# A transposed batch without its side buffer, and the order of ScalarE's work at the head of an expert stage

## The chip, the cores and the metric

The kernel runs on one core of a Trainium2 chip. The metric is the device time of one execution in microseconds, here the median of three runs. The core has five engines: TensorE (PE in the profile), VectorE (DVE), ScalarE (ACT), GpSimd (POOL) and SyncE (SP), whose queue issues all the transfers of this kernel. Each engine works through its own instructions in program order and waits at semaphores for the others.

## The reference, cut to what matters

```python
xn = layernorm(x)                                  # x: (16, 512, 128) fp32
h  = xn @ fc_w.T + fc_b
for _ in range(8):                                 # dt = 1/8
    h = h + dt * (sigmoid(alpha) * 0.5 * (adj @ h - h) + h @ w_eff - h + xn)
x  = x + h
z  = layernorm(x)
p  = softmax(z @ router_w.T)                       # 8 experts, the 2 best kept
out = z
for e in range(8):
    out = out + combine[:, e] * (gelu(z @ w1[e] + b1[e]) @ w2[e] + b2[e])
return x + out
```

## The kernel before

The 16 batches are taken in 8 groups of two (GB = 2). An iteration g first does the graph part of group g (eight Euler steps folded into products with powers of two matrices, and the second layer norm), and then the expert stage of group g - 1. Iteration 0 has no expert stage, iterations 1 to 6 are alike, iteration 7 is the last with a graph part, and after it comes the expert stage of group 7 alone. This text numbers the expert stages 1 to 8; stage k works on group k - 1.

An expert stage has 16 items, eight experts for each of the two batches. Names for item i:

- U(i): three TensorE matmuls, z times the first weights (split in a high and a low part), into one of three PSUM banks (lines 1129 to 1131).
- G(i): GELU on ScalarE into `hid` (line 610).
- S(i): VectorE multiplies by the token's routing weight into `scaled`, one of three buffers (line 989).
- H(i): ScalarE rounds `scaled` to its high part in `scs` (line 482, called by `item_high`).
- L(i): VectorE subtracts, giving the low part (line 678, called by `item_low`).
- D(i): TensorE adds w2 times both parts to the sum bank: two matmuls that need H(i) (line 1306) and one that needs L(i) (line 1313, "the low matmul").

TensorE's order is U0 to U5, D0, U6, D1 and so on (LAG = 5); U(i) for i of 3 and more waits for G(i - 3), whose bank it takes. ScalarE's order is G0 G1 H0 G2 H1 G3 H2 ... VectorE's is S0 S1 L0 S2 L1 ... `hid` has two buffers.

In between stand other things. In the stages 1 to 7 the layer norm's result z for the next group is written tile by tile: VectorE scales the four tiles of the first batch behind items 5 and 6, ScalarE those of the second batch (`scale_z`, line 592) behind items 6, 7, 8 and 9. When the last is done, SyncE writes z to memory and reads it back in blocks (lines 345 and 351); VectorE transposes these (`turn_z`, line 961) after item 15, and high and low parts go to `zT`, from which the next stage's U and the router's logits read. The second batch goes to a side buffer `zT_next`, and ScalarE copies it to `zT` (`move_zt`, line 578) at the start of the next iteration. In stage 7 nothing goes through memory: TensorE transposes z's two batches behind items 10 and 12 of its order (`Z_AT`), ScalarE and VectorE take the parts at once, and TensorE computes the logits before D13. The routing follows on VectorE, and stage 8 begins with TensorE replicating routing rows (line 1277) as soon as ScalarE has copied the result (`combT`).

VectorE turns the first batch's sum (`turn_y`, line 978) behind S11 and L10, and GpSimd then adds the residual (line 447).

Of the kernel before, what the change touches and what calls it, by code (L numbers as in the profile page):

```python
# [29 lines left out]
F32R = mybir.dt.float32r  # L30
# [5 lines left out]
P = 128  # L36
# [8 lines left out]
def build(nc, x, adj, alpha, w, d, fc_w, fc_b, router_w, w1, b1, w2, b2, comb_rows, x0_rows, z_rows, res_rows, out):  # L45
    B, N, D = x.shape
    E = router_w.shape[0]
    NT = N // P
# [12 lines left out]
    with ctx:  # L61
        def sb(name, shape, dt=FP32):
            return ctx.enter_context(nc.sbuf_tensor(name, shape, dt))

        def sem(name):
            return ctx.enter_context(nc.semaphore(name))
# [47 lines left out]
        resq = sb("resq", [P, GB, N])  # L114
        zt = sb("zt", [P, GB, N])
        zT = sb("zT", [P, 2, GB, N], F32R)
        zT_next = sb("zT_next", [P, 2, N], F32R)
        rt = sb("rt", [P, 6, T, E])
        rm = sb("rm", [P, 10, T])
        cc = sb("cc", [P, T, 4, E])  # L120
        lgT = cc[:, :, :, :].rearrange("p t k e -> p t (k e)")
        combT = sb("combT", [P, H], F32R)
        comb_out = sb("comb_out", [P, H])
        work = sb("work", [P, 5, N])
        hid = work[:, 0:2]
        scaled = work[:, 2:5]
        Lnat = work[:, 0:4]
        w12_raw = work[:, 0:4].rearrange("p (k r) n -> p k (r n)", k=2).rearrange("p k (e c) -> p k e c", c=D)
        w_raw = work[:, 4, 0:2 * P].rearrange("p (k c) -> p k c", c=P)
# [61 lines left out]
        h8_mm, x1_add = sem("h8_mm"), sem("x1_add")  # L191
        z_ready, res_ready = sem("z_ready"), sem("res_ready")
        zt_mm, zt_hi, zt_lo = sem("zt_mm"), sem("zt_hi"), sem("zt_lo")
        zt_moved = sem("zt_moved")
        z_kept, zq_in, z_turned = sem("z_kept"), [sem(f"zq_in{b}") for b in range(GB)], sem("z_turned")
        lg_mm, rt_own, rt_pre, rt_tanh, comb_ready = (sem(n) for n in ("lg_mm", "rt_own", "rt_pre", "rt_tanh", "comb_ready"))
        rep_mm = sem("rep_mm")
# [25 lines left out]
        H8_BANK = [4, 5, 6, 7]  # L223
        REP_ITEMS = [0, 2, 6, 8, 14]
        REP_BANK, REP_PE = [3, 7], 6
        Z_SCALE, Z_AT = 5, [10, 12]
        BY_PE = GROUPS - 2
        ROUTE_AT = [0, 1, 3, 4]
        UP_BANK, SUM_BANK = [4, 5, 6], [0, 1]
# [18 lines left out]

            return R * (2 * b + half)

        def zt_part(s, b):

            return zT_next[:, s, :] if b == GB - 1 else zT[:, s, b, :]

        def wait_low(engine, h, i):

# [223 lines left out]
        def _(act):  # L480
            def high(dst, src):
                return nc.scalar.activation(dst, src, ACT.Copy)  # L482
# [82 lines left out]
            def high_z(turn, b, banks=ZT_BANK):  # L565

                act.wait_ge(zt_mm, GB * turn + b + 1)
                high(zt_part(0, b), bank[banks[b]][:, :]).then_inc(zt_hi, 1)

            def high_turned_z(g, b):  # L570
                act.wait_ge(z_turned, GB * (g - 1) + b + 1)
# [2 lines left out]
            def route_tanh(h):  # L574
                act.wait_ge(rt_pre, h + 1)
                nc.scalar.activation(rm[:, 4, :], rm[:, 3, :], ACT.Tanh, scale=0.5).then_inc(rt_tanh, 1)

            def move_zt(h):

                act.wait_ge(zt_lo, GB * h + GB)  # L580
                high(zT[:, :, GB - 1, :], zT_next[:, :, :]).then_inc(zt_moved, 1)

            def copy_comb(h):

# [3 lines left out]
            def scale_z(g, b, t):  # L588
                if t == 0:
                    act.wait_ge(ln_rstd[1], 2 * g + 2)  # L590
                k = GB * t + b
                last = nc.scalar.activation(z[:, t, b, :], x1[:, t, b, :], ACT.Identity,
                                            bias=shift[:, 1, k:k + 1], scale=rstd[:, 1, k:k + 1])
                if t == NT - 1:
                    last.then_inc(z_ready, 1)
# [7 lines left out]
            def experts(h, g=None, more=False):  # L603

                for i in range(ITEMS):
                    act.wait_ge(up_mm, ITEMS * h + i + 1)
                    if i >= 2:
                        act.wait_ge(sc_ready, ITEMS * h + i - 1)
                    e = i % E
                    nc.scalar.activation(hid[:, i % 2, :], bank[UP_BANK[i % 3]][:, :], ACT.Gelu,  # L610
                                         bias=cols[:, B1_COL + e:B1_COL + e + 1]).then_inc(gelu_done, 1)
                    if i == 1 and g is None:
                        copy_comb(h)
                    if i >= 1:
                        item_high(h, i - 1)
                    if Z_SCALE < i <= Z_SCALE + NT and g is not None:
                        scale_z(g, 1, i - Z_SCALE - 1)
                    if i - 1 in Z_AT and g is not None and not more:
                        high_z(1, Z_AT.index(i - 1))
                    if i == ITEMS - 4 and not more:  # L620
                        copy_sum(h, 0)
                item_high(h, ITEMS - 1)
                if more:
                    high_turned(g + 1)
                if not more:
                    copy_sum(h, 1)
                if more:
                    for b in range(GB):
                        high_turned_z(g, b)
                if g is not None and not more:  # L630
                    route_tanh(g)

            def iteration(g, first=False, final=False):
                if not first:
                    move_zt(g - 1)
                    high_gt(g, 3, 3)
                    route_tanh(g - 1)
                for p in range(2):
                    act.wait_ge(q_ready, T * g + NT * (p + 1))
                    high(y2s[:, 0, 2 * p:2 * p + 2], Q[:, 2, 2 * p:2 * p + 2]).then_inc(y2_hi, 1)  # L640
                    if p == 1 and not first:
                        copy_comb(g - 1)
                    if p == 0 and not final:
                        scale_x0(g + 1)
                        high_x0(g + 1)
                for t in range(NT):
                    act.wait_ge(y1_add, NT * g + t + 1)
                    high(y1s[:, 0, t], y1[:, t]).then_inc(y1_hi, 1)
                if not final:
                    copy_x(g + 1)  # L650
                if first:
                    high_x0t(g + 1)
                    for k in range(2):
                        high_gt(g + 1, k, k)
                    for b in range(GB):
                        high_z(0, b, ZT_FIRST)
                    high_gt(g + 1, 2, 2)
                else:
                    experts(g - 1, g, not final)
                    if not final:  # L660
                        for k in range(3):
                            high_gt(g + 1, k, k)
# [2 lines left out]
            with act.Fori(1, GROUPS - 1) as g:  # L665
                iteration(g)
            iteration(GROUPS - 1, final=True)
            move_zt(GROUPS - 1)
            experts(GROUPS - 1)


# [1 line left out]
        def _(dve):  # L673
# [280 lines left out]

            def low_z(g, b, banks=ZT_BANK):
                dve.wait_ge(zt_hi, GB * g + b + 1)
                low(zt_part(1, b), bank[banks[b]][:, :], zt_part(0, b)).then_inc(zt_lo, 1)

            def turn_z(g, b):
                dve.wait_ge(zq_in[b], 64 * g)  # L960
# [19 lines left out]
            def scale_item(h, i, by_pe):  # L980

                dve.wait_ge(gelu_done, ITEMS * h + i + 1)
                if by_pe:
                    dve.wait_ge(rep_mm, i + 1)
                elif i in REP_ITEMS:
                    dve.wait_ge(rep_in[REP_ITEMS.index(i)], 16 * h + 16)
                if i >= 3:
                    wait_low(dve, h, i - 3)
                v.tensor_tensor(scaled[:, i % 3, :], hid[:, i % 2, :], bank[REP_BANK[i % 2]][:, :] if by_pe else rep(i),  # L989
                                ALU.mult).then_inc(sc_ready, 1)  # L990

            def item_low(h, i):
# [133 lines left out]
        def _(pe):  # L1126
# [119 lines left out]
                        if tiles[-1] == NT - 1:  # L1246
                            last.then_inc(done, 1)

            def logits(h):
                pe.wait_ge(zt_lo, GB * h + GB)  # L1250
                for b in range(GB):
                    for half in range(2):
                        first = P - R - quarter(b, half)
                        for s in range(2):
                            last = pe.matmul(bank[LG_BANK][:, 0:H], rts[:, first:first + P],  # L1255
                                             zt_part(s, b)[:, half * H:(half + 1) * H],
                                             start=(b + half + s == 0), stop=(b + half + s == 3))
                last.then_inc(lg_mm, 1)

# [21 lines left out]
            def experts(h, g=None, more=False):  # L1281

                for s in range(ITEMS + LAG):
                    if s < ITEMS:
                        b, e = s // E, s % E
                        if s >= 3:
                            pe.wait_ge(gelu_done, ITEMS * h + s - 2)
                        elif g is not None:
                            pe.wait_ge(x1_add, NT * g + s + 1)
                        elif UP_BANK[s] in OT_BANK:  # L1290
                            pe.wait_ge(out_add, 1 + GB * h)
                        if s == E:
                            pe.wait_ge(zt_moved, h + 1)
                        mm3(bank[UP_BANK[s % 3]][:, :], w1s[:, 0, e, :], w1s[:, 1, e, :],
                            zT[:, 0, b, :], zT[:, 1, b, :], True, True).then_inc(up_mm, 1)
                        if s == 1 and g is None:
                            pe.wait_ge(ct_high, h + 1)
                            replicate(h, 0)
                        if 1 <= s < REP_PE and g is None:
                            replicate(h, s)  # L1300
# [16 lines left out]
                    if s == ITEMS - 1 and not more:  # L1317
                        transpose_out(h, 0)
                    if s == ITEMS + 1 and g is not None and not more:
                        logits(g)  # L1320
                    if s >= ITEMS and more:
                        if s == ITEMS:
                            pe.wait_ge(x0_lo, GB * (g + 1) + GB)
# [91 lines left out]
```

## Time and profile before

| | |
|---|---|
| median of 3 runs | 533.34 us (532.8 to 533.89) |
| profiled execution | 534.12 us, span 532.0 us, mean granted TensorE clock 0.995 |
| TensorE busy | 517.8 us, 97% |
| VectorE busy | 439.0 us, 83% |
| ScalarE busy | 305.9 us, 57% |
| GpSimd busy | 112.0 us, 21% |
| GELU (line 610) | 128 of 0.679 us |
| high part of an item (line 482) | 132 of 0.629 us |
| low part of an item (line 678) | 132 of 0.739 us |

The span reaches from the first to the last instruction; the execution's own time has some two microseconds around it. Matmuls overlap at their ends, so TensorE's busy share says little of how close it is to its pace: the distance from one start to the next does. "L610" in a row is line 610 of the kernel. A row of a timeline has the start and the duration in microseconds, the engine, the line, the operation with output and input, the count of merged instructions, and in brackets the engine's idle time before it and who ended it.

### The profile page before, as it was taken

The page shows a single profiled execution, that of the slowest core. Times are in us where ns is not written, and L with a number is a line of the kernel's source. Part 1 is how long each engine was busy: PE and PEld are TensorE (multiplying, and loading weights), DVE is VectorE, ACT ScalarE, POOL GpSimd, SP SyncE. Part 2 cuts the span into 40 slices and gives each one's busy share as a digit, 9 for nine tenths or more (in the row PEclk, how much of TensorE's full clock was granted, in tenths as well). Part 3 has the DMA queues.
Part 4 walks back from the last instruction along what each step waited for, and adds up shares of the span by engine and source line. Part 5 has one row for each costly group of instructions (what it writes and reads, how often), then busy time and mean ns, then how long its engine had stood idle before and what let it go on. Part 6 is the DMA issues. An engine that isn't in the chain of part 4 may idle for free.

```text
span 532.0 us, 9196 instructions
## 1 busy us (share of the span) xinstructions
PE 517.8 (97%) x2799; PEld 453.6 (85%) x2799; DVE 439.0 (83%) x1012; ACT 305.9 (57%) x541; POOL 112.0 (21%) x174
## 2 busy tenths in 40 slices
PE   5999999999999999999999999999999999999796
PEld 4788997997799888998799878998899788988685
DVE  5888777779967997789967997789877996589985
ACT  6323434449635885459545884469545882159584
POOL 1204004204150412213240412222230412030100
PEclk9999999999999999999999999999999999999999
DMA  4040011099326972198327962298328841260151
GB/s 133 2 118 0 1 41 40 16 268 235 61 59 138 288 145 62 45 262 209 59 59 172 268 134 59 67 275 184 50 57 222 233 79 20 71 231 19 42 198 41
DMA packets 139359, 62.04 MB, mean 117 GB/s; under 512 B 102614, under 2 KB 133964, under 8 KB 137420
## 3 DMA queue, kind: packets, MB, share of 16 engines
q1 hardware_dynamic: 139340, 61.81, 46.7%
q8 instruction: 9, 0.15, 0.1%
q14 instruction: 10, 0.08, 0.0%
HBM read 47.90 MB, written 13.89 MB: 116 GB/s over the span
## 4 chain that ended last, share of the span: by engine, by line
PE 82%; DVE 8%; DMA 3%; ACT 2%; issue 2%; SPq 2%; POOL 1%; DVEq 0%; ACTq 0%; POOLq 0%
PE bank L1129 21%; PE bank L1131 21%; PE bank L1130 21%; PE bank L1306 10%; PE bank L1313 5%; DVE work L989 2%; DMA x0q<-x_rows 2%; DVE scs L678 1%; PE bank L1255 1%; ACT work L610 1%; DMA x_rows<-x 1%; SPq L338 1%; DVE bn L682 1%; DMA work<-in_adj_dram 1%; DVE Q L1097 1%
## 5 line engine op out<-in xcount | busy, mean ns | idle before, releaser
L678 DVE TENSOR_TENSOR scs<-work,scs 128x512 fp32r<-128x512 f32 x132 | 97.4, 739 | 1.9 <-ACT scs L482 0.5
L610 ACT ACTIVATE work<-bank,cols 128x512 f32<-128x512 f32 x128 | 86.8, 679 | 16.5 <-PE bank L1131 16.4
L482 ACT ACTIVATE scs<-work 128x512 fp32r<-128x512 f32 x132 | 83.0, 629 | 18.9 <-DVE work L989 17.5
L1306 PE MATMUL bank<-scs,w2s 128*128 128x512 f32 x256 | 80.7, 396 | 0.0
L1131 PE MATMUL bank<-M,GT 128*128 128x384 f32 x192 | 64.2, 335 | 0.0
L1129 PE MATMUL bank<-M,GT 128*128 128x384 f32 x192 | 64.2, 334 | 0.0
L1130 PE MATMUL bank<-M,GT 128*128 128x384 f32 x192 | 64.2, 334 | 0.0
L989 DVE TENSOR_TENSOR work<-work,GT 128x512 f32<-128x512 f32 x90 | 61.1, 685 | 3.2 <-issue 1.4
L423 POOL TENSOR_TENSOR mv<-bn 128x8 f32<-128x8 f32 x16 | 6.7, 418 | 240.6 <-DVE bn L682 240.6
L1306 PEld LDWEIGHTS bank<-scs,w2s 128*128 128x128 f32 x256 | 47.8, 188 | 10.8
L1129 PE MATMUL bank<-zT,w1s 128*128 128x512 f32 x128 | 52.1, 407 | 0.9 <-ACT work L610 0.4
L1313 PE MATMUL bank<-scs,w2s 128*128 128x512 f32 x128 | 51.1, 400 | 0.0
L1129 PE MATMUL bank<-LT,x0s 128*128 128x512 f32 x128 | 51.1, 399 | 0.0
L1131 PE MATMUL bank<-zT,w1s 128*128 128x512 f32 x128 | 50.8, 397 | 0.0
L1130 PE MATMUL bank<-zT,w1s 128*128 128x512 f32 x128 | 50.6, 395 | 0.0
L482 ACT ACTIVATE GT<-bank 128x512 fp32r<-128x512 f32 x36 | 21.1, 595 | 50.8 <-PE bank L1131 48.2
L1131 PE MATMUL bank<-LT,x0s 128*128 128x512 f32 x128 | 50.1, 391 | 0.0
L1130 PE MATMUL bank<-LT,x0s 128*128 128x512 f32 x128 | 49.9, 390 | 0.0
L1054 DVE TENSOR_TENSOR Q<-bank,bias 128x384 f32<-128x384 f32 x64 | 35.2, 550 | 17.6 <-PE bank L1131 17.5
L447 POOL TENSOR_TENSOR outs<-outs,resq 128x512 f32<-128x512 f32 x12 | 17.2, 1436 | 117.6 <-DVE outs L978 117.6
L678 DVE TENSOR_TENSOR GT<-bank,GT 128x512 fp32r<-128x512 f32 x36 | 24.5, 689 | 20.8 <-ACT GT L482 20.7
L1129 PEld LDWEIGHTS bank<-M,GT 128*128 128x128 f32 x192 | 36.0, 188 | 0.3
(193 smaller groups left out, 1227.5 us busy)
## 6 DMA issues: line engine op xcount, KB each, us to landing
GT<-comb_rows SPq DMA_DIRECT2D x8, 1536.0 KB, 7.1
Q<-comb_rows SPq DMA_DIRECT2D x16, 512.0 KB, 7.2
GT<-comb_rows SPq DMA_DIRECT2D x7, 1024.0 KB, 5.8
xn<-in_x_dram SPq DMA_DIRECT2D x16, 256.0 KB, 4.1
GT<-comb_rows SPq DMA_DIRECT2D x7, 512.0 KB, 4.4
res_rows<-scr SPq DMA_DIRECT2D x12, 256.0 KB, 2.6
x_rows<-x SPq DMA_DIRECT2D x12, 256.0 KB, 2.6
x0q<-x_rows SPq DMA_DIRECT2D x24, 128.0 KB, 4.0
```

The costliest lines, as they stand in the source:

```text
L423: nc.gpsimd.tensor_tensor(mv[:, n, 1, :], mean_e, mean_o, ALU.subtract)
L447: nc.gpsimd.tensor_tensor(turned, turned, resq[:, b, :], ALU.add).then_inc(out_add, 1)
L482: return nc.scalar.activation(dst, src, ACT.Copy)
L610: nc.scalar.activation(hid[:, i % 2, :], bank[UP_BANK[i % 3]][:, :], ACT.Gelu, bias=cols[:, B1_COL + e:B1_COL + e + 1]).then_inc(gelu_done, 1)
L678: return v.tensor_tensor(dst, src, hi.bitcast(FP32), ALU.subtract)
L989: v.tensor_tensor(scaled[:, i % 3, :], hid[:, i % 2, :], bank[REP_BANK[i % 2]][:, :] if by_pe else rep(i), ALU.mult).then_inc(sc_ready, 1)
L1054: v.tensor_tensor(Q[:, :, t, b, :], src, bias[:, t], ALU.add).then_inc(q_ready, 1)
L1129: pe.matmul(dst, wh, xh, start=start, stop=False)
L1130: pe.matmul(dst, wh, xl, start=False, stop=False)
L1131: return pe.matmul(dst, wl, xh, start=False, stop=stop)
L1306: pe.matmul(bank[SUM_BANK[b]][:, :], w2s[:, k, e, :], scs[:, i % RING, 0, :], start=(e == 0 and k == 0), stop=False)
L1313: pe.matmul(bank[SUM_BANK[b]][:, :], w2s[:, 0, e, :], scs[:, i % RING, 1, :], start=False, stop=(e == E - 1)).then_inc(down_mm, 1)
```

## The change

The side buffer and its copy go. In the inner iterations z's second batch is written straight into `zT`; in the last iteration, where `zT` is still being read, it goes to a part of `x0s` that is free by then. The room lets `work` grow from five to six tiles, and `hid` gets a third buffer. ScalarE's order at the head of a stage becomes G0 G1 G2 H0 H1 G3 H2 ..., and its four z tiles stand behind items 6, 8, 10 and 11.

```diff
-        zT_next = sb("zT_next", [P, 2, N], F32R)
...
-        work = sb("work", [P, 5, N])
-        hid = work[:, 0:2]
-        scaled = work[:, 2:5]
+        work = sb("work", [P, 6, N])
+        hid = work[:, 0:3]
+        scaled = work[:, 3:6]
...
-        Z_SCALE, Z_AT = 5, [10, 12]
+        Z_SCALE, Z_ACT, Z_AT = 5, [6, 8, 10, 11], [10, 12]
...
-        def zt_part(s, b):
-
-            return zT_next[:, s, :] if b == GB - 1 else zT[:, s, b, :]
+        def zt_part(s, b, last=False):
+
+            if last and b == GB - 1:
+                return x0s[:, s, 0:NT // 2].rearrange("p t b c -> p (t b c)")
+            return zT[:, s, b, :]
...
-            def move_zt(h):
-
-                act.wait_ge(zt_lo, GB * h + GB)
-                high(zT[:, :, GB - 1, :], zT_next[:, :, :]).then_inc(zt_moved, 1)
...
                     act.wait_ge(up_mm, ITEMS * h + i + 1)
-                    if i >= 2:
-                        act.wait_ge(sc_ready, ITEMS * h + i - 1)
+                    if i >= 3:
+                        act.wait_ge(sc_ready, ITEMS * h + i - 2)
                     e = i % E
-                    nc.scalar.activation(hid[:, i % 2, :], bank[UP_BANK[i % 3]][:, :], ACT.Gelu,
+                    nc.scalar.activation(hid[:, i % 3, :], bank[UP_BANK[i % 3]][:, :], ACT.Gelu,
                                          bias=cols[:, B1_COL + e:B1_COL + e + 1]).then_inc(gelu_done, 1)
                     if i == 1 and g is None:
                         copy_comb(h)
-                    if i >= 1:
+                    if i == 2:
+                        item_high(h, 0)
+                    if i >= 2:
                         item_high(h, i - 1)
-                    if Z_SCALE < i <= Z_SCALE + NT and g is not None:
-                        scale_z(g, 1, i - Z_SCALE - 1)
+                    if i in Z_ACT and g is not None:
+                        scale_z(g, 1, Z_ACT.index(i))
...
             def iteration(g, first=False, final=False):
                 if not first:
-                    move_zt(g - 1)
                     high_gt(g, 3, 3)
...
-                        if s == E:
-                            pe.wait_ge(zt_moved, h + 1)
                         mm3(bank[UP_BANK[s % 3]][:, :], w1s[:, 0, e, :], w1s[:, 1, e, :],
-                            zT[:, 0, b, :], zT[:, 1, b, :], True, True).then_inc(up_mm, 1)
+                            zt_part(0, b, g is None), zt_part(1, b, g is None), True, True).then_inc(up_mm, 1)
```

## Rows read from the trace of the kernel before

**Rows 1.** The page, busy time: us, share of the span, instructions.
```profile
PE 517.8 (97%) x2799; PEld 453.6 (85%) x2799; DVE 439.0 (83%) x1012; ACT 305.9 (57%) x541; POOL 112.0 (21%) x174
```

**Rows 2.** Timeline, TensorE, stage 2: start, duration (us), engine, line, operation.
```profile
176.14 0.40 PE L1129 MATMUL bank<-zT,w1s 128*128 128x512 f32 x1
...
179.34 0.39 PE L1131 MATMUL bank<-zT,w1s 128*128 128x512 f32 x1
179.84 0.50 PE L1129 MATMUL bank<-zT,w1s 128*128 128x512 f32 x1
...
196.23 0.49 PE L1313 MATMUL bank<-scs,w2s 128*128 128x512 f32 x1
```

**Rows 3.** Timeline, ScalarE, head of stage 2.
```profile
177.04 1.38 ACT L610 ACTIVATE work<-bank,cols 128x512 f32<-128x512 f32 x2 [1.51 <-PE bank L1131]
178.58 0.63 ACT L482 ACTIVATE scs<-work 128x512 fp32r<-128x512 f32 x1 [0.16 <-DVE work L989]
179.12 0.67 ACT L610 ACTIVATE work<-bank,cols 128x512 f32<-128x512 f32 x1
179.69 0.62 ACT L482 ACTIVATE scs<-work 128x512 fp32r<-128x512 f32 x1
```

**Rows 4.** Timeline, VectorE, stage 2.
```profile
177.85 1.31 DVE L989 TENSOR_TENSOR work<-work,GT 128x512 f32<-128x512 f32 x2 [0.16 <-ACT work L610]
179.25 0.69 DVE L678 TENSOR_TENSOR scs<-work,scs 128x512 fp32r<-128x512 f32 x1
179.85 0.68 DVE L989 TENSOR_TENSOR work<-work,GT 128x512 f32<-128x512 f32 x1
...
189.94 0.69 DVE L678 TENSOR_TENSOR scs<-work,scs 128x512 fp32r<-128x512 f32 x1
190.76 0.69 DVE L989 TENSOR_TENSOR work<-work,GT 128x512 f32<-128x512 f32 x1
...
194.38 1.79 DVE L678 TENSOR_TENSOR scs<-work,scs 128x512 fp32r<-128x512 f32 x1
```

**Rows 5.** Timeline, GpSimd, stage 2.
```profile
194.03 1.58 POOL L447 TENSOR_TENSOR outs<-outs,resq 128x512 f32<-128x512 f32 x1 [9.80 <-DVE outs L978]
```

**Rows 6.** Timeline, ScalarE, middle of stage 2.
```profile
187.65 0.63 ACT L482 ACTIVATE scs<-work 128x512 fp32r<-128x512 f32 x1
...
189.67 0.48 ACT L592 ACTIVATE scr<-Q,shift,rstd 128x128 f32<-128x128 f32 x1
190.05 0.67 ACT L610 ACTIVATE work<-bank,cols 128x512 f32<-128x512 f32 x1
```

**Rows 7.** Timeline, TensorE, stages 1 and 6.
```profile
116.81 0.40 PE L1129 MATMUL bank<-zT,w1s 128*128 128x512 f32 x1
...
137.16 0.51 PE L1313 MATMUL bank<-scs,w2s 128*128 128x512 f32 x1
...
412.84 0.40 PE L1129 MATMUL bank<-zT,w1s 128*128 128x512 f32 x1
...
432.93 0.48 PE L1313 MATMUL bank<-scs,w2s 128*128 128x512 f32 x1
```

**Rows 8.** Timeline, TensorE, stage 7 and head of stage 8.
```profile
487.45 0.60 PE L1263 MATMUL bank<-ident,scr 128*128 128x128 f32 x4
...
502.19 0.73 PE L1277 MATMUL bank<-combT,pick 128*128 128x256 f32 x4 [2.10 <-ACT combT L482]
```

**Rows 9.** Windows: us, busy and count by engine, granted clock, DMA share, GB/s.
```profile
502.20:506.30 4.10, 4.10 (x15) 3.50 (x16) 3.46 (x6) 2.25 (x4) 2.39 (x1) 0.58 0.26 72
```

**Rows 10.** Timeline, SyncE's queue, stage 2.
```profile
192.47 4.04 SPq L351 DMA_DIRECT2D x0q<-z_rows  x8
```

**Rows 11.** Timeline, VectorE, behind stage 2.
```profile
200.49 1.30 DVE L961 STREAM_TRANSPOSE zt<-x0q 128x512 f32<-128x512 f32 x2
```

**Rows 12.** Timeline, ScalarE, around the copy of line 581.
```profile
209.72 1.06 ACT L482 ACTIVATE zT<-zT_next 128x1024 fp32r<-128x1024 f32 x1
211.49 0.60 ACT L482 ACTIVATE GT<-bank 128x512 fp32r<-128x512 f32 x1 [0.70 <-PE bank L1131]
```

More of the change, by code:

```diff
@@ L193, in build @@
         zt_mm, zt_hi, zt_lo = sem("zt_mm"), sem("zt_hi"), sem("zt_lo")
-        zt_moved = sem("zt_moved")
         z_kept, zq_in, z_turned = sem("z_kept"), [sem(f"zq_in{b}") for b in range(GB)], sem("z_turned")
@@ L567, in high_z @@
                 act.wait_ge(zt_mm, GB * turn + b + 1)
-                high(zt_part(0, b), bank[banks[b]][:, :]).then_inc(zt_hi, 1)
+                high(zt_part(0, b, turn == 1), bank[banks[b]][:, :]).then_inc(zt_hi, 1)
             def high_turned_z(g, b):
@@ L667, in _ @@
             iteration(GROUPS - 1, final=True)
-            move_zt(GROUPS - 1)
             experts(GROUPS - 1)
@@ L956, in low_z @@
                 dve.wait_ge(zt_hi, GB * g + b + 1)
-                low(zt_part(1, b), bank[banks[b]][:, :], zt_part(0, b)).then_inc(zt_lo, 1)
+                last = banks is ZT_BANK
+                low(zt_part(1, b, last), bank[banks[b]][:, :], zt_part(0, b, last)).then_inc(zt_lo, 1)
             def turn_z(g, b):
@@ L988, in scale_item @@
                     wait_low(dve, h, i - 3)
-                v.tensor_tensor(scaled[:, i % 3, :], hid[:, i % 2, :], bank[REP_BANK[i % 2]][:, :] if by_pe else rep(i),
+                v.tensor_tensor(scaled[:, i % 3, :], hid[:, i % 3, :], bank[REP_BANK[i % 2]][:, :] if by_pe else rep(i),
                                 ALU.mult).then_inc(sc_ready, 1)
@@ L1247, in horner, with logits @@
                             last.then_inc(done, 1)
-            def logits(h):
+            def logits(h, final=False):
                 pe.wait_ge(zt_lo, GB * h + GB)
@@ L1255, in logits @@
                             last = pe.matmul(bank[LG_BANK][:, 0:H], rts[:, first:first + P],
-                                             zt_part(s, b)[:, half * H:(half + 1) * H],
+                                             zt_part(s, b, final)[:, half * H:(half + 1) * H],
                                              start=(b + half + s == 0), stop=(b + half + s == 3))
@@ L1319, in experts @@
                     if s == ITEMS + 1 and g is not None and not more:
-                        logits(g)
+                        logits(g, True)
                     if s >= ITEMS and more:
```

## The prediction

> **What bounds the kernel now.** I read the page's busy times first, then TensorE's timeline through one whole expert stage, then the timelines of ScalarE, VectorE and GpSimd beside it. TensorE is busy 517.8 of 532.0 us [rows 1], but that includes overlapping ends. The pace is in the starts: U0 starts at 176.14 and the last of U0 to U4's fifteen matmuls at 179.34 [rows 2], 14 steps of 0.229 us. TensorE is late where a step is longer, and I looked for such steps. In every expert stage 1 to 6 I found the same two. U5 begins at 179.84, not at 179.34 + 0.23 = 179.57: 0.27 us lost, and its first matmul takes 0.50 us instead of 0.39, another 0.11. The second is the low matmul of D11 (L1313) at 196.23, with 0.49 us again [rows 2].
>
> The first has a plain cause: U5 needs G2, and G2 (179.12 to 179.79) stands behind H0, which itself had to wait for S0 [rows 3]. The second needs VectorE: L11 starts at 194.38 and takes 1.79 us, to 196.17 [rows 4], and the matmul starts 0.06 later. L11 is long because GpSimd adds the residual from 194.03 to 195.61, released by VectorE's transpose just before [rows 5]. The transpose follows L10, so this overlap travels with VectorE's chain. VectorE works from L0 to L11 almost without a pause: scale and low part follow each other at 0.60 us (179.25 to 179.85); the one hole is before S10, at 190.76 instead of 189.94 + 0.60 = 190.54, so 0.22 us [rows 4], for G10, which ends at 190.05 + 0.67 [rows 6]. So the later limit of a stage is L11, whatever TensorE gains at U5. From U0 to D11's low matmul takes 20.35 us in stage 1 and 20.09 in stage 6 [rows 7]; the six are 20.35, 20.09, 20.35, 20.25, 20.14 and 20.09, mean 20.21. After it TensorE keeps its pace up to the next stage's U5.
>
> **The third GELU buffer and the new order.** From GELU 3 on ScalarE's order is what it was (G3, H2, G4, H3, ...), and H(i-2) had already waited for S(i-2), so the old condition on the second buffer never held G(i) longer. The only effect is at the head: G0 G1 G2 H0 H1 instead of G0 G1 H0 G2 H1. U2's last matmul starts 8 x 0.229 after 176.14, at 177.97, and takes 0.40; G2 can start at about 178.41 instead of 179.12, right behind G1 (177.04 + 1.38 = 178.42) [rows 2, 3]. It ends at 179.1, so U5 starts on time: gain 0.38 us at U5. H0, in exchange, starts a GELU later. From G2 to H1 the step is 0.57 (179.12 to 179.69) [rows 3], so H0 starts at 178.98 and ends 0.63 later at 179.61. L0 followed H0's end by 0.04 (178.58 + 0.63 = 179.21, L0 at 179.25) [rows 3, 4]; it now starts at 179.65, 0.40 later. VectorE has only S0 and S1 before it, done at 179.16 [rows 4], and S2 stands behind L0 in its order though G2 is ready early. So the whole chain L0, S2, L1, ... starts 0.40 later.
>
> **The moved z tiles.** ScalarE's four tiles go from items 6, 7, 8, 9 to 6, 8, 10, 11. A tile costs ScalarE 0.38 (189.67 to 190.05) [rows 6]. From H7 to G10 took 2.40 (187.65 to 190.05) [rows 6], with two tiles; with one it is 2.02, so G10 no longer holds S10: 0.22 back. Then G10, H9, a tile, G11 take 0.57 + 0.54 + 0.38 = 1.49, so G11 ends 2.02 + 1.49 + 0.68 = 4.19 after H7 starts, that is some 4.9 after S7 starts; VectorE would want it 8 x 0.60 = 4.8 after S7. S11 waits 0.1. Net of the two: 0.12 back.
>
> In stage 2, L11 then ends 0.40 - 0.12 = 0.28 later and D11's low matmul starts at 20.37 after U0. The head of the chain is now set by G2 and not by S0, so I expect 20.37 in all six stages against a mean of 20.21: 6 x 0.16 = 1.0 us slower. The 6 x 0.38 at U5 all goes into the longer wait at D11. Bounds: if S10's and S11's waits both vanish, 6 x 0.06 = 0.4; if neither does, 6 x 0.4 = 2.4.
>
> The last tile also ends 3.0 us later (it is two items of 1.2 and more behind), and with it the write of z to memory. The eight reads that turn z start at 192.47 and take 4.04 to issue [rows 10]; they move to 195.5 to 199.5. VectorE turns z at 200.49 and 201.14 [rows 11], so some 1.7 us lie between issue and the second use, where there were 4.7. A transfer in here may hold the second transpose by some tenths; the logits that need z come 7 us later (207.6), so I take nothing. Queued behind these reads on SyncE are the stores of the first output batch, which nobody waits for before the next stage.
>
> **The buffer removed.** The copy takes 1.06 us on ScalarE, but the high part behind it starts at 211.49 after 0.70 us of waiting for TensorE [rows 12]. It is hidden seven times and worth nothing; in stage 8 it stands before G0, long before the routing is ready. Should it have been a cover for something, 1.06 us per use is the most it could give back, and the 0.70 says it gives none. TensorE's removed wait had been met eight items before.
>
> **The last two stages.** In stage 7 TensorE transposes z's second batch behind D7, at 487.45 [rows 8]. The last tile ended 1.6 before that and will end 3.1 later, at about 488.9, so TensorE stops there for some 1.7 us. By itself this is hidden: the routing is the path, and TensorE waits 2.10 us for it at 502.19 [rows 8]. But ScalarE there has the copies of the transposed z and of the first sum between its GELUs and no idle time from H7 on, and one tile moves from before H7 to behind it. VectorE's chain begins 0.5 late (H0 again; here S0 was quicker than elsewhere) and waits 0.38 more at G12. So the routing ends 0.9 later: from 0.4 (the head alone) to 1.3 (two tiles). In stage 8, U2 stands behind the first replicated rows, so H0 behind G2 waits longer; TensorE needs S3 for the sixth replicated row, and I take 0.2 us, from 0 to 0.6.
>
> **Sum.** 1.0 + 0.9 + 0.2 = 2.1 us slower. The profiled execution took 534.12 us for its span of 532.0; it becomes 536.2. The median of the runs is 533.34, 0.8 below, so I forecast **535.4** (0.4% slower). No change means within 0.2% or 1.07 us, about what this kernel's measurement can tell.
>
> **Rivals.**
> (A) The forecast: the chain L0 to L11 is the limit and starts later. 0.58.
> (B) Faster: D11's wait moves with TensorE instead of with L11, so that the gap at U5 is truly gained. 6 x 0.38 = 2.3, less 1.1 in the last stages: 1.2 us faster, 532.1. It decides where D11's low matmul starts: if in stage 2 it comes before 20.0 us after U0, B holds. Against it: the start follows L11's end by 0.06. For it: the wait at U5 is real and the same in all stages. The Trainium skill (Perfetto Trace Analysis, Identifying Performance Opportunities) says that the same gap repeated on the engine that should be saturated can mean too few buffers; by that rule the third buffer gives these 2.3 us. The trace agrees on the gap, but shows a later one behind it. 0.08.
> (C) No change: VectorE swallows most of the 0.40, or z's tiles cost stage 7 only the head. 0.4 + 0.4 = 0.8 slower, 534.1. A z tile of VectorE that already waits for GpSimd in stages 1, 3 and 4 speaks for it, and the late ScalarE in stage 7 against it. 0.22.
> (D) The stop of 1.7 us in stage 7 halves TensorE's clock. After the 2.10 us wait the granted clock over 4.1 us was 0.58 [rows 9], so part of it at 1.2 GHz: (1 - 0.58) x 4.1 = 1.7 us of TensorE's time. The logits would come 1.7 later with 0.6 of slack: 1.1 more, 536.5. The Trainium skill (TensorE: Matmul & The Clock Gate, Part 1) has the throttled clock as the default that only activity lifts, which would make such a stop dear. The stop is shorter than that wait, so I hold it for unlikely. 0.12.
>
> **Range and chances.** A's own range is 534.4 to 536.6. With C's lower part and D, and the unknown costs, 532.9 to 537.3. Faster has B's 0.08; no change has C's 0.22; slower A and D, 0.70.
>
> **What would show it.** Right: U5 without a gap and its first matmul at 0.39 us; G2 directly behind G1; L0 0.40 later after U0; no wait before S10; D11's low matmul near 20.37 after U0 in all six stages, just behind L11, with a longer wait; a stop of TensorE before the second transposes of z in stage 7; the first replicated row 0.9 later than the stages' own delay explains. Wrong: D11's low matmul earlier than 20.0 after U0, or an L11 of 0.7 us because GpSimd's addition falls elsewhere, which would take 1.1 us off every stage's wait.

## The result and the profile after

The changed kernel takes 535.24 us (median of 6 runs, 534.98 to 535.8), the kernel before 533.25 (6 runs, 532.79 to 533.89). The ratio is 1.0037 with a 95% interval of 1.0026 to 1.0047: 0.4% slower, 2.0 us. The forecast was 535.4.

TensorE's timeline in stage 2 of the changed kernel (start, duration, line, operation; the lines have moved: a matmul of U is now L1125 to L1127, D's low matmul L1307):

```profile
175.30 0.40 PE L1125 MATMUL bank<-zT,w1s 128*128 128x512 f32 x1
...
178.50 0.39 PE L1127 MATMUL bank<-zT,w1s 128*128 128x512 f32 x1
178.73 0.39 PE L1125 MATMUL bank<-zT,w1s 128*128 128x512 f32 x1
...
188.86 0.50 PE L1125 MATMUL bank<-zT,w1s 128*128 128x512 f32 x1
...
195.66 0.50 PE L1307 MATMUL bank<-scs,w2s 128*128 128x512 f32 x1 [0.26 <-DVE scs L673]
```

U0 starts at 175.30. The last matmul of U4 starts at 178.50 and U5 follows at 178.73, one step of 0.23 later, and takes 0.39 us: the gap of [rows 2] is gone. D11's low matmul comes at 195.66, 20.36 after U0, where it was 20.09; it now waits so long that the profile lists the wait. A row in between shows a new small delay: U12's first matmul, at 188.86 and 0.50 us long, starts 0.06 after G9 ends (188.13 + 0.67, in ScalarE's rows below). The profile's chain of work that ended last has changed with it. Its shares of the span by engine:

```profile
PE 67%; DVE 19%; issue 6%; ACT 5%; POOL 1%; DMA 1%; DVEq 0%; SPq 0%; ACTq 0%; POOLq 0%
```

TensorE had 82% of this chain before, VectorE 8%. It now goes through VectorE's low parts (line 673, 9% of the span), which had 1%.

ScalarE, VectorE and GpSimd beside it, in the same stage:

```profile
176.20 2.06 ACT L605 ACTIVATE work<-bank,cols 128x512 f32<-128x512 f32 x3 [1.51 <-PE bank L1127]
178.16 1.14 ACT L482 ACTIVATE scs<-work 128x512 fp32r<-128x512 f32 x2
179.20 0.68 ACT L605 ACTIVATE work<-bank,cols 128x512 f32<-128x512 f32 x1
...
187.21 0.63 ACT L482 ACTIVATE scs<-work 128x512 fp32r<-128x512 f32 x1 [0.51 <-DVE work L985]
...
188.13 0.67 ACT L605 ACTIVATE work<-bank,cols 128x512 f32<-128x512 f32 x1
...
190.70 0.68 ACT L605 ACTIVATE work<-bank,cols 128x512 f32<-128x512 f32 x1
```

```profile
177.01 1.31 DVE L985 TENSOR_TENSOR work<-work,GT 128x512 f32<-128x512 f32 x2 [0.23 <-ACT work L605]
178.81 0.69 DVE L673 TENSOR_TENSOR scs<-work,scs 128x512 fp32r<-128x512 f32 x1 [0.48 <-ACT scs L482]
179.42 0.69 DVE L985 TENSOR_TENSOR work<-work,GT 128x512 f32<-128x512 f32 x1
...
189.51 0.68 DVE L673 TENSOR_TENSOR scs<-work,scs 128x512 fp32r<-128x512 f32 x1
190.11 0.68 DVE L985 TENSOR_TENSOR work<-work,GT 128x512 f32<-128x512 f32 x1
190.72 0.68 DVE L673 TENSOR_TENSOR scs<-work,scs 128x512 fp32r<-128x512 f32 x1
191.41 0.69 DVE L985 TENSOR_TENSOR work<-work,GT 128x512 f32<-128x512 f32 x1
...
193.82 1.78 DVE L673 TENSOR_TENSOR scs<-work,scs 128x512 fp32r<-128x512 f32 x1
```

```profile
193.48 1.58 POOL L447 TENSOR_TENSOR outs<-outs,resq 128x512 f32<-128x512 f32 x1 [10.89 <-DVE outs L974]
```

ScalarE runs three GELUs in one piece (176.20, three in 2.06 us) and then the high parts of items 0 and 1. Counted from U0, H0 starts at 2.86 instead of 2.44, and VectorE, which had S1 done at 178.32, is idle for 0.48 us before L0. L0 starts 3.51 after U0 instead of 3.11 [rows 4]: the 0.40 of the forecast. The hole before S10 is gone (189.51, 190.11, 190.72 are 0.60 apart); the one before S11 is new (191.41 instead of 191.32). L11 starts 0.28 later after U0 and takes 1.78 us, beside GpSimd's addition as before.

The six stages are now alike. Stage 1 and stage 6, U0 and D11's low matmul:

```profile
115.95 0.40 PE L1125 MATMUL bank<-zT,w1s 128*128 128x512 f32 x1
...
136.31 0.50 PE L1307 MATMUL bank<-scs,w2s 128*128 128x512 f32 x1 [0.27 <-DVE scs L673]
...
412.72 0.40 PE L1125 MATMUL bank<-zT,w1s 128*128 128x512 f32 x1
...
433.10 0.50 PE L1307 MATMUL bank<-scs,w2s 128*128 128x512 f32 x1 [0.27 <-DVE scs L673]
```

20.36 and 20.38 us, against 20.35 and 20.09 in [rows 7]. Over six iterations, from stage 1's U0 to stage 7's, the sum is 472.07 - 115.95 = 356.12 us, where it was 471.89 - 116.81 = 355.08: 1.04 us more.

Stage 7 and the head of stage 8, TensorE:

```profile
472.07 0.40 PE L1125 MATMUL bank<-zT,w1s 128*128 128x512 f32 x1
...
487.10 0.40 PE L1307 MATMUL bank<-scs,w2s 128*128 128x512 f32 x1
489.11 0.66 PE L1259 MATMUL bank<-ident,scr 128*128 128x128 f32 x4 [1.61 <-ACT scr L587]
...
503.25 0.73 PE L1273 MATMUL bank<-combT,pick 128*128 128x256 f32 x4 [1.44 <-ACT combT L482]
...
507.30 0.50 PE L1273 MATMUL bank<-combT,pick 128*128 128x256 f32 x2 [0.57 <-DVE work L985]
```

Behind D7 (487.10) TensorE stops for 1.61 us, until ScalarE's last z tile is done. The first replicated row comes 503.25 - 472.07 = 31.18 after stage 7's U0; it was 502.19 - 471.89 = 30.30. That is 0.88 more. In stage 8 there is a new wait of 0.57 us at 507.30, for S2.

TensorE's granted clock after both stops (windows, columns as in [rows 9]):

```profile
489.20:500.00 10.80, 10.11 (x53) 8.25 (x54) 10.03 (x23) 7.00 (x14) 0.00 (x0) 1.00 0.08 24
503.30:507.00 3.70, 3.43 (x17) 2.41 (x17) 2.36 (x5) 2.29 (x4) 2.39 (x1) 1.00 0.29 80
```

It stays at full speed, also in the stretch at the head of stage 8 where it was 0.58 before.

The reads that turn z, on SyncE's queue, and VectorE's use of them:

```profile
194.61 4.04 SPq L351 DMA_DIRECT2D x0q<-z_rows  x8
```

```profile
199.92 1.30 DVE L957 STREAM_TRANSPOSE zt<-x0q 128x512 f32<-128x512 f32 x2
```

The reads are issued 2.98 us later after U0 than in [rows 10], and VectorE's two transposes still start without a wait and follow L15 as in [rows 11].

### The profile page after: what moved, and what is told of

It is laid out like the page before. It is cut to its first block, busy times and chain, and to the rows that moved or that the text cites. A ratio compares the mean times of both kernels' runs of the same rounds, so it can differ in the third digit from the quotient of the medians.

```text
span 532.8 us, 9172 instructions
## 1 busy us (share of the span) xinstructions
PE 515.5 (97%) x2799; PEld 450.7 (85%) x2799; DVE 437.9 (82%) x1012; ACT 299.6 (56%) x533; POOL 107.6 (20%) x174
## 4 chain that ended last, share of the span: by engine, by line
PE 67%; DVE 19%; issue 6%; ACT 5%; POOL 1%; DMA 1%; DVEq 0%; SPq 0%; ACTq 0%; POOLq 0%
PE bank L1127 19%; PE bank L1125 19%; PE bank L1126 19%; DVE scs L673 9%; DVE work L985 5%; PE bank L1300 4%; PE bank L1307 2%; ACT scs L482 2%; ACT work L605 2%; PE bank L1251 1%; DVE scr L687 1%; DVE outs L974 1%; PE bank L1153 1%; POOL rstd L438 1%; DVE bn L677 1%
## 5 line engine op out<-in xcount | busy, mean ns | idle before, releaser
L1127 PE MATMUL bank<-M,GT 128*128 128x384 f32 x192 | 64.2, 335 | 0.0
L1125 PE MATMUL bank<-M,GT 128*128 128x384 f32 x192 | 64.2, 334 | 0.0
L1307 PE MATMUL bank<-scs,w2s 128*128 128x512 f32 x128 | 51.2, 400 | 1.6 <-DVE scs L673 1.6
L1125 PE MATMUL bank<-LT,x0s 128*128 128x512 f32 x128 | 51.1, 400 | 0.0
L1127 PE MATMUL bank<-LT,x0s 128*128 128x512 f32 x128 | 50.1, 392 | 0.0
L1125 PE MATMUL bank<-zT,w1s 128*128 128x512 f32 x120 | 48.3, 402 | 0.0
L1127 PE MATMUL bank<-zT,w1s 128*128 128x512 f32 x120 | 47.1, 393 | 0.0
L1126 PE MATMUL bank<-zT,w1s 128*128 128x512 f32 x120 | 46.9, 391 | 0.0
```

The source lines that it names most:

```text
L1125: pe.matmul(dst, wh, xh, start=start, stop=False)
L1126: pe.matmul(dst, wh, xl, start=False, stop=False)
L1127: return pe.matmul(dst, wl, xh, start=False, stop=stop)
L1307: pe.matmul(bank[SUM_BANK[b]][:, :], w2s[:, 0, e, :], scs[:, i % RING, 1, :], start=False, stop=(e == E - 1)).then_inc(down_mm, 1)
```

## The experiments

The first four were timed against 532.90 us, the median of 29 runs of the kernel before, the other four against 533.02 (23 runs). The changed kernel itself was timed only against the 533.25 above, so a difference from its 535.24 us carries the 0.2 to 0.4 us by which these medians of one kernel differ. The iteration times from the profiles do not.

**The old order at the head.**

```diff
-                    if i == 2:
-                        item_high(h, 0)
-                    if i >= 2:
+                    if i >= 1:
                         item_high(h, i - 1)
```

> The changed kernel with ScalarE's old order at the head of every stage (G0 G1 H0 G2 H1), all else as changed: third GELU buffer there but unused at the head, z tiles behind items 6, 8, 10, 11. My theory (H0 behind G2 starts VectorE's chain 0.40 us later): L0 at 3.1 to 3.2 us after U0 again instead of 3.51, the 0.38 us gap at U5 back, D11's low matmul near 20.1 after U0 instead of 20.36, so 6 x 0.26 = 1.5 us less in stages 1 to 6, 0.5 less in stage 7, and 0.2 in stage 8: 2.2 us faster than the changed kernel, 533.0, the same as before. Rival (the gain at U5 is real, the loss sits in z's moved tiles): slower than the changed kernel by 6 x 0.38 = 2.3, 537.5.

Measured: 533.09 us, 1.0002 of before (0.9993 to 1.0011). VectorE, then TensorE:

```profile
177.33 1.31 DVE L983 TENSOR_TENSOR work<-work,GT 128x512 f32<-128x512 f32 x2
178.72 0.69 DVE L671 TENSOR_TENSOR scs<-work,scs 128x512 fp32r<-128x512 f32 x1
```

```profile
179.32 0.50 PE L1123 MATMUL bank<-zT,w1s 128*128 128x512 f32 x1
...
487.72 0.55 PE L1257 MATMUL bank<-ident,scr 128*128 128x128 f32 x3 [0.81 <-ACT scr L587]
```

L0 starts right behind S1, 3.10 after U0 (175.62), and U5's first matmul is back at 0.50 us behind its gap. D11's low matmul starts 20.14 after U0. The six iterations take 354.76 us, against 355.08 before and 356.12 in the changed kernel. So this order, not the moved tiles, carries the loss of stages 1 to 6. The rival with 537.5 is out. The third GELU buffer is still there, and the gap at U5 is back: it was the new order that closed it, not the buffer by itself. In stage 7 the stop is still there but shorter (0.81 us, 487.72), and the first replicated row comes 30.67 after U0, 0.51 earlier than in the changed kernel.

**The old z tiles.**

```diff
-        Z_SCALE, Z_ACT, Z_AT = 5, [6, 8, 10, 11], [10, 12]
+        Z_SCALE, Z_ACT, Z_AT = 5, [6, 7, 8, 9], [10, 12]
```

> The changed kernel with ScalarE's z tiles behind items 6, 7, 8, 9 again. My theory: S10 waits 0.2 us for G10 again instead of S11 0.1 for G11, so D11's low matmul comes 0.1 later, at 20.47 after U0: 6 x 0.1 = 0.6 slower; in stage 7 the stop of 1.6 us before z's second transposes is gone and the routing comes 0.4 earlier: net 0.2 to 0.3 slower, 535.5, no measurable difference. Rival (the moved tiles are the loss): back to 533.3.

Measured: 535.91 us, 1.0052 of before (1.0039 to 1.0065). TensorE, stage 2's U0 and D11, and the first replicated row:

```profile
175.62 0.40 PE L1125 MATMUL bank<-zT,w1s 128*128 128x512 f32 x1
...
196.10 0.50 PE L1307 MATMUL bank<-scs,w2s 128*128 128x512 f32 x1 [0.30 <-DVE scs L673]
...
503.70 0.50 PE L1273 MATMUL bank<-combT,pick 128*128 128x256 f32 x2 [2.90 <-ACT combT L482]
```

D11's low matmul starts 20.48 after U0, 0.12 later than with the moved tiles. The six iterations take 356.76 us, 0.64 more than in the changed kernel. The first replicated row comes 503.70 - 472.92 = 30.78 after stage 7's U0, 0.40 earlier. Both sizes are the forecast's. The time is not: 0.7 us above the changed kernel, where 0.2 to 0.3 were expected. The low clock returned in stage 8, after a wait of 2.90 us for the routing (granted 0.65 from 503.7 to 508.6, with matmuls 0.43 us apart), and from the first replicated row to the last D it took 24.81 us instead of 24.39. The expectation had not priced these 0.4. With the new order in place, the moved tiles are thus a gain of 0.64 us in the six iterations and a loss of 0.40 in stage 7.

**Only the buffers.** The two edits above together. What stays of the change is the side buffer and its copy taken away, and the third GELU buffer, without the order that would use it.

> Both undone: the changed kernel with the old head order and the old z tiles, so that only the side buffer, its copy and TensorE's wait for it are gone. My theory (the copy was hidden): as before, 533.25 within 0.5 us, and the starts after U0 of all items as before. Rival (removing seven copies of 1.06 us helps): up to 7 us faster, 526.

Measured: 533.23 us, 1.0002 of before (0.9993 to 1.001). D11's low matmul starts 20.09 to 20.30 after U0 in the six stages, as before. The side buffer's copy was hidden: taking it away is worth nothing within the noise of 0.1%, and neither is the third GELU buffer by itself.

**The addition after L15, in the changed kernel.**

```diff
                 pool.wait_ge(resq_in, 64 * h + 64)
+                if b == 0:
+                    pool.wait_ge(sc_lo, ITEMS * h + ITEMS)
```

> The changed kernel, but GpSimd's residual addition for the first batch also waits for L15, so that it no longer runs beside L11. My theory (L11 is the later limit of a stage, and 1.1 of its 1.79 us is the addition): L11 takes 0.69, D11's low matmul follows its high ones at 19.9 to 20.0 after U0 instead of 20.36 and U5's gain is kept, 6 x 0.5 = 3.1 us faster than the changed kernel: 532.1, 0.2% faster than before. Rival (D11's low matmul waits for something else): no change, 535.2.

Measured: 532.13 us, 0.9987 of before (0.9979 to 0.9996). L11 on VectorE, then TensorE:

```profile
193.63 0.68 DVE L675 TENSOR_TENSOR scs<-work,scs 128x512 fp32r<-128x512 f32 x1
```

```profile
175.11 0.40 PE L1127 MATMUL bank<-zT,w1s 128*128 128x512 f32 x1
...
194.59 0.63 PE L1302 MATMUL bank<-scs,w2s 128*128 128x512 f32 x2
195.06 0.40 PE L1309 MATMUL bank<-scs,w2s 128*128 128x512 f32 x1
195.29 0.40 PE L1127 MATMUL bank<-LT,x0s 128*128 128x512 f32 x1
```

L11 takes 0.68 us, and D11's low matmul (195.06) follows its high ones by 0.47 without a wait, 19.95 after U0. One iteration lasts 58.82 to 58.84 us instead of 59.35. L11 was the later limit, and 1.1 us of it came from GpSimd's addition running beside it.

**The addition after L15, in the kernel before.** The same edit.

> The kernel before with one edit: GpSimd's residual addition for the first batch also waits for L15. My theory: L11 takes 0.69 and D11's low matmul follows its high ones at 20.08 after U0 in every stage, with U5's gap of 0.38 still there. The loss at D11 in the profile of before (0.1 to 0.28 in each of six stages, 1.1 together) goes: 532.1, 0.2% faster than before. The same edit on the changed kernel brought 3.1, so this tells that the third buffer's gain was hidden behind L11. Rival (the addition's overlap slows VectorE everywhere alike): 3 us faster here too, 530.2.

Measured: 532.38 us, 0.9989 of before (0.9979 to 0.9998). TensorE in stage 2:

```profile
174.91 0.40 PE L1131 MATMUL bank<-zT,w1s 128*128 128x512 f32 x1
...
178.12 0.39 PE L1133 MATMUL bank<-zT,w1s 128*128 128x512 f32 x1
178.61 0.50 PE L1131 MATMUL bank<-zT,w1s 128*128 128x512 f32 x1
...
195.00 0.40 PE L1315 MATMUL bank<-scs,w2s 128*128 128x512 f32 x1
```

U5's gap stands (178.12 to 178.61), and D11's low matmul starts 20.09 after U0. The iterations take 58.97 to 59.03 us. With the addition out of the way the changed iterations are 0.15 us shorter than the old ones on average; with it they were 0.17 longer (59.35 against a mean of 59.18). The head order is a gain that VectorE's chain turned into a loss. The rival (3 us here too) is out: by the medians the edit gained 0.6 us here, by the six iterations 1.2.

**The old order in the stages 7 and 8 alone.**

```diff
-                    if i == 2:
+                    if i == 2 and more:
                         item_high(h, 0)
-                    if i >= 2:
+                    if i >= (2 if more else 1):
                         item_high(h, i - 1)
-                    if i in Z_ACT and g is not None:
-                        scale_z(g, 1, Z_ACT.index(i))
+                    z_act = Z_ACT if more else [6, 7, 8, 9]
+                    if i in z_act and g is not None:
+                        scale_z(g, 1, z_act.index(i))
```

> The changed kernel, with the old head order and z tiles behind items 6, 7, 8, 9 in stages 7 and 8 alone. My theory: TensorE's stop before z's second transposes goes, the first replicated row comes 30.3 after stage 7's U0 instead of 31.2, stage 8 has H0 in time (0.2) but TensorE waits over 2 us for the routing again and falls to the low clock for some us (0.4 back): 0.7 faster than the changed kernel, 534.5. Stages 1 to 6 stay at 59.35 us each. Rival (the loss is all in stages 1 to 6): no change, 535.2.

Measured: 534.39 us, 1.0026 of before (1.0016 to 1.0035). TensorE in stage 7 and at the head of stage 8:

```profile
487.68 0.60 PE L1260 MATMUL bank<-ident,scr 128*128 128x128 f32 x4
...
502.39 0.74 PE L1274 MATMUL bank<-combT,pick 128*128 128x256 f32 x4 [2.07 <-ACT combT L482]
```

The second transposes of z follow D7 without a stop, and the first replicated row comes 502.39 - 472.11 = 30.28 after stage 7's U0, as before. TensorE waits 2.07 us for the routing, and the low clock is back. The iterations stay at 59.33 to 59.36. The time is 0.9 us under the changed kernel's 535.24, but by the two ratios (1.0026 and 1.0037) and by the two profiles, from stage 1's U0 to the last D, it is 0.6. So of the 2.0 us some 0.6 to 0.9 lie in the last two stages, and the rest mostly in the six iterations.

**Both remedies.** The late addition and the old order in stages 7 and 8.

> The late addition and the old order in stages 7 and 8 together. If both parts of the loss are independent, the gains add: 3.1 and 0.7 under the changed kernel's 535.2, so 531.4, with 58.82 us for each of the six iterations.

Measured: 531.22 us, 0.9963 of before (0.9949 to 0.9977); the iterations take 58.82 us. The two parts add up as expected.

**And the tiles behind items 6, 7, 10, 11.** Both remedies and, in stages 1 to 6, this:

```diff
-        Z_SCALE, Z_ACT, Z_AT = 5, [6, 8, 10, 11], [10, 12]
+        Z_SCALE, Z_ACT, Z_AT = 5, [6, 7, 10, 11], [10, 12]
```

> As the one before, with the z tiles of stages 1 to 6 behind items 6, 7, 10, 11. ScalarE is idle before H7, so the tile at 7 costs nothing there, and G9 comes 0.38 earlier; U12, which began 0.14 late behind G9 and ran 0.1 longer, is on time. 6 x 0.25 = 1.5 us less: 58.57 us for each iteration, 529.9. If ScalarE's tile instead delays G8 so that U11 or S8 waits, no gain: 531.4.

Measured: 529.99 us, 0.994 of before (0.9924 to 0.9955): 0.6% faster, the best of all. TensorE, stage 2's U0, U5 (3.43 after it, no gap), D11's low matmul and the next U0:

```profile
175.56 0.40 PE L1128 MATMUL bank<-zT,w1s 128*128 128x512 f32 x1
...
178.99 0.39 PE L1128 MATMUL bank<-zT,w1s 128*128 128x512 f32 x1
...
195.28 0.40 PE L1310 MATMUL bank<-scs,w2s 128*128 128x512 f32 x1
...
234.16 0.40 PE L1128 MATMUL bank<-zT,w1s 128*128 128x512 f32 x1
```

The iterations take 58.57 to 58.60 us. D11's low matmul comes 19.72 after U0, and TensorE's list of waits has none left in stages 1 to 6. An iteration is 0.39 us shorter than with the late addition alone in the kernel before (58.98): the whole loss at U5, 0.38, has come back.

## Why the prediction was right

**The head.** G2 directly behind G1, H0 0.42 and L0 0.40 later, U5 on time: each as worked out. The old order alone gave the time before back (533.09 against 532.90), so the step from head to loss is shown, not only argued. What remains open is how much of it needed the third buffer, since no run has the new order with two. In [rows 3] H0 starts at 178.58, after its wait for S0, and G2 with only two buffers would have to wait for the same S0. In H0's place it would end at 178.58 + 0.67 = 179.25, before the 179.57 at which U5 was due. By this estimate two buffers would have closed the gap too.

**L11 as the later limit.** Forecast 20.37 after U0 in all six stages, measured 20.36 to 20.39, sum 1.04 us for a forecast of 1.0. The late addition took the wait away in both kernels. In the kernel before, the limit was only just reached in some stages: D11's 20.09 in stages 2 and 6 is also what it takes without the addition, and L11 cost those stages only a matmul 0.1 us longer. The term's upper bound was too high: 6 x 0.4 starts from a stage of 20.09, while the mean was 20.21. The run with the old z tiles, where S10's wait stays, shows what it should have been: 20.48, and 356.76 - 355.08 = 1.7 us over the six.

Rival B is refuted: the gap at U5 closed and the time rose. The Trainium skill's rule on repeated gaps (Perfetto Trace Analysis, Identifying Performance Opportunities) says that such a gap can mean too few buffers. These runs do not bear it out: the third buffer alone left the gap where it was. The new order closed it, and the gain showed only once the later wait was gone too.

**The moved tiles.** Forecast 0.12 per stage; the old tiles cost 0.12 per stage at D11. What I left out was U12: it starts 0.14 late behind G9 in the changed kernel, and its first matmul is 0.1 longer. It cost nothing there, since D11 waited longer anyway, and became 0.23 us per iteration once that wait was gone.

**The last two stages.** 0.88 for the forecast 0.9 in stage 7, and the runs bear out both parts, 0.5 for the head (0.51 with the old order) and 0.4 for the tiles (0.40 with the old tiles). In stage 8 the term was off: 0.2 slower was forecast, and from the first replicated row to the last D it took 527.64 - 503.25 = 24.39 us where it had taken 526.78 - 502.19 = 24.59. H0's delay is there: with the clock at full speed in both, the old head took 24.16 (the run with the old order) and the new one 24.39; with the low clock in both, 24.66 (only the buffers) and 24.81 (the old z tiles). But the clock stayed high in the changed kernel's profile. TensorE's work behind its stop lies closer to the routing's end, and its wait there shrank from 2.10 to 1.44 us. That gave 0.4 back, which the prediction had not foreseen. That the shorter wait is the reason is likely and not certain: one profile with a wait of 2.10 us kept the high clock too (last section). Rival D had the sign wrong: after 1.61 us of standstill the granted clock stayed at 1.00. The Trainium skill (TensorE: Matmul & The Clock Gate, Part 1) has the low clock as the default after an idle window; the profile with the stop agrees in so far as no low clock came after a stop that short.

**No change (C)** needed VectorE to swallow most of the 0.40. It swallowed 0.12 net in stage 2. The waits of VectorE's own z tiles for GpSimd in stages 1, 3 and 4 did vanish, but that was in the sum, since all six stages were taken to the same 20.37.

**Where luck helped.** From stage 1's U0 to the last D, the two profiles differ by 1.04 + 0.88 - 0.20 = 1.7 us, for a forecast of 2.1. The medians differ by 2.0. That 535.24 came within 0.2 us of 535.4 is therefore partly luck: the sign of the term of stage 8 was wrong, and the remaining 0.3 us is not placed by any run.

**The profile's own span** rose only 0.8 us (532.0 to 532.8). The difference lies ahead of stage 1: its U0 is at 115.95 instead of 116.81. In the profiled execution of before, the first nine matmuls of 512 columns, from 10.84 to 14.79, started some 0.43 us apart (the first two 0.56); in that of the changed kernel they started 0.23 apart. In the profiles of all ten kernels stage 1's U0 lies at 115.89 to 116.96.

## What to carry to other kernels

Before paying for an earlier start, look for the last wait in the same stage and ask which engine's chain it ends; here the engine that gained (TensorE) was not the one that set the stage's end (VectorE), and the gain was taken from the head of VectorE's chain. A start that follows the end of the same producer by 0.06 us is a limit, even where the list of waits does not show it. And a change of an engine's order should be priced separately in the last repetition, where other work stands in between.

## What the runs showed that I had not expected

- After a wait of 2.07 to 2.90 us for the routing, six of seven profiled executions show TensorE's matmuls 0.43 us apart for some microseconds; one, after 2.10 us, does not. After 1.43 to 1.49 us none of three does. The record of all executions agrees. Each has a mean granted clock over its span, and the six with the low stretch have 0.995 or 0.996. Of the three kernels with the short wait, none of 29 executions has 0.997 or less; of the others, 60 of 104 do. So with the longer wait the low stretch comes in some executions of a kernel and not in others, and no run here tells what decides it.
- The low stretch costs only 0.4 to 0.6 us. In the profiles with the old head, it takes 24.59 to 24.73 us from the first replicated row to the last D with the low stretch, and 24.16 without. In the four kernels with at least five executions of either kind, the medians of the two kinds are 0.4 to 0.6 us apart. At full speed S2 holds TensorE up for 0.35 to 0.57 us, and in the low stretch this wait is gone.
- At the very start, the windows view prints a granted clock of 1.00 for the kernel before while its matmuls stand 0.43 us apart. The trace has no record of the clock there: its first one, full speed, begins at 14.7 us, just where the pace changes to 0.23. In the changed kernel it begins at 9.7, before the first of these matmuls. All ten traces fit: where the first record begins between 13.6 and 15.1 us (five of them), five to nine steps of 0.43 stand before it; where it begins by 10.2 there are none. No run here tells what sets that moment; it differs between kernels whose start is the same.
- GpSimd's addition of 1.58 us stretches VectorE's subtraction beside it, with two inputs in SBUF, from 0.68 to 1.78 us. VectorE's multiplication that had started 0.2 us ahead of the addition took 0.65, as it does with the addition out of the way.
